# Attention 0 of a two-layer kernel: values once per tile instead of once per unit, scores first in each unit

## The reference, cut to what matters

```python
x = _rmsnorm(hidden_states, ln_w)                       # hidden_states = layernorm(x)
q = einsum('bqd,hd->bqh', x, wq)                        # 32 heads of 32
k = einsum('bkd,hd->bkh', ctx, wk); v = einsum('bkd,hd->bkh', ctx, wv)   # 8 key heads, each used by 4 query heads
scores = einsum('bhqd,bhkd->bhqk', q, k) / sqrt(32)
attn = softmax(scores); out = einsum('bhqk,bhkd->bhqd', attn, v)
```

## Time and profile before

| | us |
|---|---|
| median of three executions | 1440.12 |
| the profiled execution | 1441.05 |
| its span in the profile | 1439.2 |
| first attention, its 128 units | 183.5 to 683 |
| busy: PE / PEld | 1342.5 / 1047.9 |
| busy: DVE / ACT / POOL | 898.6 / 690.7 / 280.2 |

### The profile page before, as it was taken

One profiled execution on the slowest core, in us unless ns is written; L12 is line 12 of the kernel. 1 busy time (PEld: TensorE's weight loads), 2 busy tenths in 40 slices (PEclk: granted clock), 3 DMA queues, 4 the chain that ended last, 5 costly groups with the idle time before them and its releaser, 6 DMA issues. The chain is left out here.

```text
span 1439.2 us, 26120 instructions
## 1 busy us (share of the span) xinstructions
PE 1342.5 (93%) x9815; PEld 1047.9 (73%) x9815; DVE 898.6 (62%) x1451; ACT 690.7 (48%) x1762; POOL 280.2 (19%) x333
## 2 busy tenths in 40 slices
PE   6999799999999999988899999999978999999498
PEld 6998788989898888865788888888854545554244
DVE  4353377776777777665332336667856677887797
ACT  4222076766766677674211111102225666665396
POOL 0010001011010101011010113324222444443323
PEclk9999899999999999999899999999988999999889
DMA  6752464545525455564645356111235455444123
GB/s 220 258 162 77 100 139 106 144 123 131 140 74 141 108 144 137 143 175 129 199 167 197 121 194 234 59 44 50 76 90 132 109 118 118 112 101 90 55 95 143
DMA packets 137315, 185.44 MB, mean 129 GB/s; under 512 B 31703, under 2 KB 101463, under 8 KB 137200
## 3 DMA queue, kind: packets, MB, share of 16 engines
q1 hardware_dynamic: 137200, 183.82, 45.0%
HBM read 88.57 MB, written 35.29 MB: 86 GB/s over the span
## 5 line engine op out<-in xcount | busy, mean ns | idle before, releaser
L1151 ACT ACTIVATE a_prob<-a_psS,a_negmax 128x256 f32<-128x256 f32 x512 | 237.2, 484 | 153.3 <-DVE a_negmax L1063 153.2
L1063 DVE TENSOR_REDUCE a_negmax<-a_psS 128x4 f32<-128x1024 f32 x128 | 154.2, 1205 | 68.8 <-PE a_psS L956 67.0
L931 PE MATMUL a_psQ<-a_xT_hi,wide 128*128 128x256 f32 x912 | 170.8, 288 | 1.1 <-DVE a_q_lo L1058 0.8
L1378 PE MATMUL m_psY<-wide,m_a_hi 128*128 128x512 f32 x512 | 159.9, 394 | 6.8 <-DVE m_a_lo L1426 6.8
L1378 PE MATMUL m_psY<-w_ffn,m_a_hi 128*128 128x512 f32 x512 | 158.3, 390 | 0.0
L966 PE MATMUL a_psT<-ident,a_prob 128*128 128x128 f32 x1024 | 137.3, 278 | 13.8 <-issue 5.8
L931 PEld LDWEIGHTS a_psQ<-a_xT_hi,wide 128*128 128x128 f32 x912 | 138.7, 189 | 9.9 <-issue 5.7
L966 PEld LDWEIGHTS a_psT<-ident,a_prob 128*128 128x128 f32 x1024 | 116.2, 143 | 23.4 <-issue 12.9
L1168 ACT COPY a_probT<-a_psT 128x512 f32<-128x512 f32 x208 | 115.9, 610 | 35.5 <-PE a_psT L966 34.4
L931 PE MATMUL a_psQ<-a_xT_lo,wide 128*128 128x256 f32 x456 | 127.4, 279 | 0.0
L881 POOL COPY a_recip<-a_recip_head 128x256 f32<-128x256 f32 x64 | 25.6, 400 | 520.5 <-DVE a_recip_head L1114 520.5
(11 more groups left out here) (241 smaller groups left out, 2636.1 us busy)
## 6 DMA issues: line engine op xcount, KB each, us to landing
a_q_stack<-a_q_hi SPq DMA_DIRECT2D x128, 128.0 KB, 2.6
a_q_stack<-a_q_lo SPq DMA_DIRECT2D x128, 128.0 KB, 2.5
b_q_stack<-b_q_hi SPq DMA_DIRECT2D x128, 128.0 KB, 2.4
c_raw<-lay_ctxT SPq DMA_DIRECT2D x16, 512.0 KB, 4.7
rows<-in_x SPq DMA_DIRECT2D x8, 1024.0 KB, 6.4
scratch_o<-a_oT SPq DMA_DIRECT2D x16, 512.0 KB, 3.0
m_x<-in_x SPq DMA_DIRECT2D x8, 1024.0 KB, 6.2
scratch_x<-m_x SPq DMA_DIRECT2D x8, 1024.0 KB, 5.1
```

What stands on the lines that cost most here:

```text
L931: last = nc.tensor.matmul(bank[:, 0:S], w[:, kt, t * P:(t + 1) * P], a[:, kt, :], start=(kt == 0 and w is wq.hi and a is xT_hi), stop=(kt ...
L1063: nc.vector.tensor_reduce(negmax[:, n % 2, :], psS[:, bank:bank + 2, :].rearrange("p a (j k) -> p (a j) k", k=S), AX_X, ALU.max, negate=Tr ...
L1151: last = nc.scalar.activation(prob[:, n % 2, j, :], psS[:, 2 * (n % 2) + j // 2, (j % 2) * S:(j % 2 + 1) * S], ACT.Exp, bias=negmax[:, n % ...
L1378: last = nc.tensor.matmul(psY[:, 2 * t + h, :], a[:, u, kt, rows_t], m[:, kt, cols], start=(kt == 0 and a is a_hi and m is w.hi), stop=(kt ...
```

## The change

Three things. `scores(n + 2)` is issued ahead of `transposes(n)`, directly behind the wait for `exp_done`. `values` is called once per tile, in every second unit (behind the transposes of units 2, 4, ..., 14, and at the end of the batch), and then handles both units of the tile, 32 instructions on end, and the two R transposes. For that the transposed probabilities of the even unit have to be kept longer: `probT` has three buffers instead of two, the even units using buffers 0 and 1 in turn and the odd units buffer 2. VectorE and ScalarE keep their order; only the buffer that their copies write is another.

```diff
--- before.py
+++ after.py
@@ -707,6 +707,7 @@
     QUAD = KT // 2
     BANK0_DVE = set(range(XFILLS + 1, UNITS, 2))
     QUAD_DMAS = JH0 * 4
+    PROBS = TT + 1
 
     COPY_STEP = {f + 1: f for f in range(XFILLS)}
     for t in range(KT - 1):
@@ -727,11 +728,16 @@
         k_stack = sb("k_stack", [P, 2, NKV0, S], F32R)
         v0 = sb("v0", [P, 2, TT, KV0])
         prob = sb("prob", [P, 2, JH0, S])
-        probT = sb("probT", [P, 2, TT, JH0, P])
+        probT = sb("probT", [P, PROBS, TT, JH0, P])
         negmax = sb("negmax", [P, 2, JH0])
         sums = sb("sums", [P, 2, TT, JH0])
         recip_head = sb("recip_head", [P, 2, TT, JH0])
         recip = sb("recip", [P, 2, TT, JH0, HD0])
+
+        def probs_of(n):
+
+            return PROBS - 1 if n % TT else n // TT % (PROBS - 1)
+
         recipT = sb("recipT", [P, S])
         oT = sb("oT", [P, KT, S])
         psS = es.enter_context(nc.psum_tensor("a_psS", [P, 4, HALF_N], F32))
@@ -959,7 +965,6 @@
                 last.then_inc(scores_full, 1)
 
             def transposes(b, n):
-                pe.wait_ge(exp_done, UNITS * b + n + 1)
                 for kt in range(TT):
                     pe.wait_ge(psT_copied[kt], UNITS * b + n + 1)
                     for j in range(JH0):
@@ -967,24 +972,23 @@
                                                    prob[:, n % 2, j, kt * P:(kt + 1) * P], ident[:, :])
                     last.then_inc(psT_full[kt], 1)
 
-            def values(b, u, n):
-                t, qb = n // TT, n % TT
-                if qb == 0:
-                    pe.wait_ge(o_ready, KT * b + t + 1)
+            def values(b, u, t):
+
+                pe.wait_ge(o_ready, KT * b + t + 1)
                 for kt in range(TT):
-                    pe.wait_ge(psT_copied[kt], UNITS * b + n + 2)
-                for kt in range(TT):
-                    for j in range(JH0):
-                        head = (t // REP0) * JH0 + j
-                        nc.tensor.matmul(psO[j * HD0:(j + 1) * HD0, 0, qb * P:(qb + 1) * P],
-                                         v0[:, u, kt, head * HD0:(head + 1) * HD0], probT[:, n % 2, kt, j, :],
-                                         start=(kt == 0), stop=(kt == TT - 1))
-                if qb == TT - 1:
-                    pe.wait_ge(recip_ready, KT * b + t + 1)
-                    for s in range(TT):
-                        last = nc.tensor.transpose(psO[:, 1, s * P:(s + 1) * P],
-                                                   recip[:, t % 2, s, :, :].rearrange("p j c -> p (j c)"), ident[:, :])
-                    last.then_inc(psO_full, 1)
+                    pe.wait_ge(psT_copied[kt], UNITS * b + TT * t + TT + 1)
+                for qb in range(TT):
+                    for kt in range(TT):
+                        for j in range(JH0):
+                            head = (t // REP0) * JH0 + j
+                            nc.tensor.matmul(psO[j * HD0:(j + 1) * HD0, 0, qb * P:(qb + 1) * P],
+                                             v0[:, u, kt, head * HD0:(head + 1) * HD0],
+                                             probT[:, probs_of(TT * t + qb), kt, j, :], start=(kt == 0), stop=(kt == TT - 1))
+                pe.wait_ge(recip_ready, KT * b + t + 1)
+                for s in range(TT):
+                    last = nc.tensor.transpose(psO[:, 1, s * P:(s + 1) * P],
+                                               recip[:, t % 2, s, :, :].rearrange("p j c -> p (j c)"), ident[:, :])
+                last.then_inc(psO_full, 1)
 
             for f in range(XFILLS):
                 transposed_x(0, 0, f, True)
@@ -1017,19 +1021,20 @@
                     b = 2 * i + u
                     more = not (final and u == 1)
                     for n in range(UNITS):
-                        transposes(b, n)
+                        pe.wait_ge(exp_done, UNITS * b + n + 1)
                         if n + 2 < UNITS:
                             scores(b, i, u, n + 2)
                         elif more:
                             scores(b + 1, i + u, 1 - u, n + 2 - UNITS)
-                        if n:
-                            values(b, u, n - 1)
+                        transposes(b, n)
+                        if n and n % TT == 0:
+                            values(b, u, n // TT - 1)
                         if more:
                             query_step(b + 1, 1 - u, n)
                         else:
                             for quarter, kt in update_steps.get(n, ()):
                                 update_part(quarter, kt)
-                    values(b, u, UNITS - 1)
+                    values(b, u, KT - 1)
 
             with pe.Fori(0, PAIRS - 1) as i:
                 body(i, False)
@@ -1106,7 +1111,7 @@
                             split(b + 1, COPY_STEP[n])
                         if n in BANK0_DVE:
                             dve.wait_ge(psT_full[0], UNITS * b + n + 1)
-                            nc.vector.tensor_copy(probT[:, n % 2, 0, :, :],
+                            nc.vector.tensor_copy(probT[:, probs_of(n), 0, :, :],
                                                   psT[:, 0, :].rearrange("p (j q) -> p j q", j=JH0)).then_inc(psT_copied[0], 1)
                         if n % 2:
                             t = n // 2
@@ -1165,7 +1170,7 @@
                             if kt == 0 and n in BANK0_DVE:
                                 continue
                             act.wait_ge(psT_full[kt], UNITS * b + n + 1)
-                            nc.scalar.copy(probT[:, n % 2, kt, :, :],
+                            nc.scalar.copy(probT[:, probs_of(n), kt, :, :],
                                            psT[:, kt, :].rearrange("p (j q) -> p j q", j=JH0)).then_inc(psT_copied[kt], 1)
                         if n + 2 < UNITS:
                             exponentials(b, n + 2)
```

## The result

The kernel after takes 1433.83 us (median of 17 executions, 1431.48 to 1438.04); the kernel before, timed with it, 1440.12 (17 executions, 1436.34 to 1443.00). The ratio is 0.9960, 95% interval 0.9951 to 0.9969: 0.4% faster, clear of no change, and 0.3 us above the 1433.5 that were forecast. A second set of seven executions gave 1433.29 beside 1440.32, ratio 0.9958 (0.9944 to 0.9973). The profiled execution after took 1431.94 us, with a span of 1430.2.

A forecast was written before the change was run, and what follows sets the result against it. TensorE bounds the first attention on average, but only units 5 to 15 can gain. Batches 0 to 5 give 5.2 us, batch 6 1.5, first stretches 0.2, batch 7 -0.3: 6.6 less, median 1433.5, range 1430 to 1436.5.

The forecast's parts named there:

- What bounds the kernel, and where: First attention: ScalarE busiest in units 0 to 4 (14.5 of 16.35 us), TensorE in units 5 to 15 (44.9 of 47.85).
- The cost of each step: TensorE's time per unit: odd units 2.77 us (before 3.53), even units 4.11 (before 3.70), 0.35 saved per pair.
- What is late next: Query waits on VectorE's split: 0.43 us in unit 7, 0.56 more in 13, 0.22 in 10; 1.2 per batch.
- Unit 10's wait: Query of unit 10 waits 0.22 us for the split, since VectorE comes late from unit 9.
- Units 5 and 11: No statistics ahead; the split ends by 1.3 us, just inside 1.35: no wait, at worst 0.1.
- Batch 6: No normalisation, but a masked sum in unit 6; unit 7's query waits 0.54 us more, leaving 1.5 of 2.07 gained.
- The last batch: Batch 7, 40-column products instead of the query: waits for VectorE's update copy hide gains; -0.3 us, between -1.5 and +1.
- The jump of the loop: TensorE's idle time at the loop's jump, 3.1 us twice, stays.
- The clock: Lower granted clock for 3.4 us behind the jump and unit 10's idle time in the last batch; 1.5 us either way.
- Cover holds: Rival: no waits in units 7, 10 and 13 because VectorE runs earlier; 14.4 us gained, 1425.7; chance 0.12.
- VectorE eats it all: Rival: splits late in all four odd units that have one, 8 us lost, 1441; chance 0.22, wholly or in part.
- The loss lies in V itself: Rival: TensorE drains between V's halves, V costs 1.33 us, not 1.02; 9 us slower, 1449; chance 0.12 with other losses.

The follow-up runs named there:

- the third experiment: Kernel after, with VectorE's statistics, normalisation and masked sum ahead of `normalise_o` and GpSimd's root one tile earlier: 1424.92 us, ratio 0.9899.

## Why the prediction was right

*What bounds the kernel, and where.* Right. The split of a batch into a stretch of ScalarE and one of TensorE carried the whole estimate: the first stretch is 16.31 against 16.35, the second 0.9 shorter, where 0.35 per tile on 64 tiles would have been 22 us.

*The cost of each step.* S 0.49 (said 0.48), T before V 1.07 (1.02), V of two units 1.01 (1.02), odd unit 2.76 to 2.77 (2.77), even unit 4.11 to 4.12 (4.11). The unknown, T straight before query products, was taken as 0.87 and is 0.87. T before V was 0.05 low and the twelve query products behind R 0.05 high, which cancels. The rule of the Trainium skill's "TensorEngine Tiling (Array Packing)", Key Properties, that a change of mode drains the engine, fits the traces: 0.17 and 0.20 us idle, before V and behind it, once per tile now. By it alone the kernel would have come to 1426; it came there only when the third experiment took the waits away.

*What is late next.* Right in mechanism, place and size for the two that matter: the query of unit 7 starts at 1.84 in its unit (said 1.78), that of unit 13 at 2.11 (said 2.04); 0.06 and 0.07 late. Unit 10's wait, put at 0.22, is 0.04: I had let the maximum gain 0.11 there, where back to back it follows the reciprocal by 0.11 instead of 0.30, and the query's own place is 2.74, not 2.69. Units 5 and 11 don't wait. Sum per batch 0.49 + 0.62 + 0.04 = 1.15 instead of 1.2. The waits of the query on the split were to grow by about 8 us in all: they have grown by 7.2, which the list shows as 4.2 to 8.8, since the changes of width were in it. Batch 6: 1.4 us gained in its second stretch, said 1.5.

*The last batch.* Wrong, by 1.7 us, and outside the -1.5 to +1 that it was given. The step that failed is the sentence "the waits of the trace show no TensorE wait on a DMA in this stage, and I count nothing". That a wait isn't in the trace says that there was slack, not how much. It was 0.57 us, less than the 0.87 by which that same paragraph moves S; the landing, 1.0 us later, took the rest. The last batch lost 2.0 us (said 0.3), of which 1.5 are this wait. Of the other 0.5 no run shows the cause.

*The jump of the loop.* Said to stay at 3.1 us twice. It is 2.77 and 2.64 here:

```profile
308.09 0.93 PEld L962 LDWEIGHTS a_psS<-a_k_stack,a_q_stack 128*128 128x128 f32 x4 [2.77 <-issue]
```

In the second profiled execution of the kernel after it is 2.65 and 3.08, and over all traces 2.6 to 3.3, so part of this is scatter.

*The clock.* Said to be worth 1.5 us either way; it was worth 1.3 in favour. In the stage it fell for 3.4 us twice in the kernel after (at 308.0 and 652.7) and three times in the kernel before (310.6, 436.9 and 658.8). Batch 4 is the difference: its first stretch was 16.69 us before, behind a fall, and 15.35 after, without one. Whether that is luck or comes of the change stays open. In the two other traces that have the kernel after in these batches (the second profiled one and the one without the table) batch 4 was spared as well; in the one other trace with TensorE's order of before, it was not. Batch 2, behind the other jump, was hit in all five.

*The sum.* The stage took 6.85 us less, where 6.6 were forecast; term by term (forecast in brackets) batches 0 to 5 in their second stretches 5.0 (5.2), batch 6 1.4 (1.5), the first stretches without batch 4's 0.4 (0.2), the second stretch of the last batch -2.1 (-0.3), and, not in the forecast, the jumps 0.8 and batch 4's clock 1.3. The terms that the mechanism gives are right to 0.2 us each. The medians differ by 6.3. That the sum is right to 0.3 us is luck: about 1.8 us too little in the last batch stand against 2.1 that nobody had counted.

*The rivals.* "Cover holds" (1425.7) was not what the change does, but what VectorE's order could make of it: the third experiment, 1424.9. Its condition was named wrongly as VectorE running earlier; R is no earlier, as the text said, and it is the work behind R that had to move ahead of it. "VectorE eats it all": the sentence of the Trainium skill's "TensorEngine Tiling (Array Packing)", PSUM Bottleneck, that emptying the banks may become the bound, bears here on two units of 16 only, and there it is a matter of order, not of throughput: VectorE is busy 30.8 of the 43.9 us, and the third experiment takes the waits away with the same work. "The loss lies in V itself": V's 32 instructions run through in 1.01 us, with no idle time between the two halves of `psO`.

## What to carry to other kernels

A gain per repetition counts only where its engine sets the pace, so read the stretch's other engines first. Where another engine sets it, what counts is how little work stands behind the instruction that waits, even if the total grows. When an engine gets shorter between two waits, the cover of what it waited for gets shorter too: take each wait's last cover from the trace, one by one, DMA landings included, since a wait with slack doesn't show in any list (here 0.57 us of slack, and 1.5 us of wait once it was used up). And where the change leaves the other engine a gap, look at what stands behind the gap in its order: moving it in front was worth more here (8 to 9 us) than the change (6 us), and nothing without it. What is moved brings its own waits along, as the statistics did with the load of x.

## What the runs showed of the hardware

A change between full-width and 32-column products costs, in the kernel after, 0.17 us of idle on the way in and 0.20 on the way out, idle time that nothing ended, and the 8 transposes ahead of it take 1.07 us instead of 0.87. On the way from the 40-column products of the last batch back to full width it is 0.41 (idle ahead of T). 32 matmuls of 32 columns into two halves of one bank run on without a gap, 0.11 us for each four. Transfers of 128 KB land 2.3 to 3.1 us behind their issue in the other batches, and 5 to 6 us behind a megabyte of table in the last. Behind a jump the stretch at the lower clock made the first stretch of a batch of the kernel after 16.6 to 16.8 us instead of 15.35. At the last two changes of stage the lower clock lasts 6.8 us each in some executions and 10.2 in others, with the same instructions, and the part behind the stage takes some 2 us more where it is 10.2: as much as several of the differences weighed here.
